# A second load of x under the gathered codes: the sum is made by the gathering DMA and copied by ScalarE instead of added by VectorE, and the orders of all engines are laid out anew

## The reference, cut to what matters

```
x = x + code(gn(x))          # layer 0: nearest of 1024 codes: argmin of the distance, then take(emb.T, index)
x = x + rows(gn(x))          # layer 1: sigmoid attention inside each row of 64 tokens
x = x + gate(gn(x)) * gn(x)  # layer 2: softmax over all 4096 tokens of an outer product, then a sigmoid gate
x = x + lin(gn(x))           # layer 3: linear attention with 4 heads, projection, layer norm
```

## Time and profile before

| | |
|---|---|
| median of three runs | 5602.64 us |
| profiled execution | span 5601.4 us from the first to the last instruction; the page gives no other time of it |
| TensorE matmul | 5252.2 us busy, 94% |
| VectorE | 4106.3 us, 73% |
| ScalarE | 3978.2 us, 71% |
| GpSimd | 1936.0 us, 35% |
| mean granted TensorE clock | 0.966 of full speed |
| mean DMA rate | 38 GB/s |

### The profile page before, as it was taken

The page is one execution under the profiler, slowest core; times in us unless marked ns, Lnnn a source line. Parts: engine busy times, 40 slices in busy tenths (PEclk is TensorE's granted clock), DMA queues, the critical chain, the costliest instruction groups (busy, mean ns, idle before and its releaser), DMA issues.

```text
span 5601.4 us, 113931 instructions
## 1 busy us (share of the span) xinstructions
PE 5252.2 (94%) x44520; PEld 2737.7 (49%) x44520; DVE 4106.3 (73%) x8674; ACT 3978.2 (71%) x6023; POOL 1936.0 (35%) x1594
## 2 busy tenths in 40 slices
PE   7799999999999999999999999999999999999996
PEld 3436445363553645446364453645436454463624
DVE  8467777776777777677777777777677777777726
ACT  1467867677785877868677675877858678686795
POOL 3225243342423424233352423424234242433403
PEclk9799999999999999999999999999999999999997
DMA  2010201102011020201102011020110102011000
GB/s 86 9 37 11 68 25 52 37 6 72 20 61 31 13 67 15 64 28 35 48 11 70 23 57 33 15 64 17 61 31 20 61 13 67 26 47 40 7 31 31
DMA packets 163253, 211.22 MB, mean 38 GB/s; under 512 B 13217, under 2 KB 146081, under 8 KB 162721
## 3 DMA queue, kind: packets, MB, share of 16 engines
q1 hardware_dynamic: 138144, 136.79, 7.6%
q0 software_dynamic: 24576, 67.14, 4.1%
HBM read 136.78 MB, written 67.11 MB: 36 GB/s over the span
## 4 chain that ended last, share of the span: by engine, by line
PE 66%; ACT 13%; DVE 11%; issue 6%; POOL 2%; DMA 1%; ACTq 0%; DVEq 0%; SPq 0%; POOLq 0%
PE PS L1195 33%; PE PS L1372 15%; PE PS L1363 6%; ACT n_x L529 3%; DVE stats L849 2%; PE PS L1471 2%; PE PS L1229 2%; PE PS L1253 2%; PE PS L1306 2%; ACT big L601 2%; ACT xin L529 2%; DMA quant_H<-emb_t,idx 1%; ACT work L568 1%; ACT attn L578 1%; ACT soft L601 1%
## 5 line engine op out<-in xcount | busy, mean ns | idle before, releaser
L601 ACT ACTIVATE big<-PS 128x1024 f32<-128x1024 f32 x1376 | 1365.8, 1024 | 460.3 <-PE PS L1363 398.9
L601 ACT ACTIVATE soft<-PS 128x1024 f32<-128x1024 f32 x672 | 676.2, 1024 | 353.9 <-PE PS L1363 346.3
L416 POOL DMA_INDIRECT quant_H<-emb_t,idx x512 | 487.4, 952 | 976.2 <-DVE idx L873 781.2
L1195 PE MATMUL PS<-e_hi,n_hi 128*128 128x512 f16 x2048 | 780.2, 381 | 17.3 <-DVE m L867 9.5
L1195 PE MATMUL PS<-e_hi,n_lo 128*128 128x512 f16 x2048 | 776.7, 379 | 0.0
L1195 PE MATMUL PS<-e_lo,n_hi 128*128 128x512 f16 x2048 | 776.7, 379 | 0.0
L1372 PE MATMUL PS<-big,w 128*4 128x512 f32 x5504 | 756.5, 638 | 0.0
L849 DVE BATCH_NORM_STATS2 stats<-XT 128x6 f32<-128x512 f32 x1024 | 651.7, 683 | 14.5 <-POOL XT L432 4.6
L873 DVE FIND_INDEX8 idx<-m,work 128x8 uint32<-128x1024 f32 x512 | 622.1, 1219 | 0.0
L1363 PE MATMUL PS<-rhs,lhs 12*128 12x512 bf16 x4096 | 557.6, 395 | 61.7 <-ACT big L601 38.8
L867 DVE CUSTOM_DVE_ANT_0 work<-PS,e_bias,m 128x512 f32<-128x512 f32 x512 | 384.0, 750 | 213.2 <-PE PS L1195 189.5
(11 more groups left out here) (208 smaller groups left out, 10799.7 us busy)
## 6 DMA issues: line engine op xcount, KB each, us to landing
xin<-x SPq DMA_DIRECT2D x128, 512.0 KB, 3.9
out<-yout SPq DMA_DIRECT2D x128, 512.0 KB, 2.9
quant_H<-emb_t,idx POOLq DMA_INDIRECT x512
XT<-emb SPq DMA_DIRECT2D x1, 1024.0 KB, 6.2
XT<-wh SPq DMA_DIRECT2D x1, 256.0 KB, 5.8
XT<-wqv SPq DMA_DIRECT2D x1, 256.0 KB, 5.8
XT<-wk SPq DMA_DIRECT2D x1, 128.0 KB, 5.8
w_sb<-w SPq DMA_DIRECT2D x1, 128.0 KB, 5.3
```

The source lines that it names most:

```text
L416: nc.gpsimd.indirect_dma_start(quant[:, g % 2, u, :], None, emb_t, bass.IndirectOffsetOnAxis(ap=idx[:, t % (2 * GT), 0:1], axis=0),).then_ ...
L601: nc.scalar.activation(E[h % 3][:, z * 1024:(z + 1) * 1024], bank(2 * z, 2), ACT.Exp).then_inc(exped.sem, 1)
L1195: ins = mm(dst, a, b, start=first and j == 0, stop=last and j == 2)
```

## The change

SyncE loads each group of x a second time, straight into `quant` (`x_again`). The gathering DMA adds the code rows to what lies there instead of writing over it. TensorE turns the sum as it turned the codes, and ScalarE copies the bank over `XT`; VectorE's `add0` is gone. GpSimd's gather now waits, at the first tile of a group, for the second load (`again`), and no longer for `l0_turned`; that wait is SyncE's. All lists are laid out anew, but TensorE's and GpSimd's for image 0 keep their order, and VectorE's for image 0 only loses `add0`.

```
+        again = [sem(f"again{s}") for s in range(2)]
 @block.sync
+            def x_again(im, g):
+                if g >= 2:
+                    sp.wait_ge(*l0_turned.after(im, 2 * g - 3))
+                elif im == 1:
+                    sp.wait_ge(*l1_outed.after(0, 2 * NG - 1))
+                elif im > 1:
+                    sp.wait_ge(*f_zed.after(im - 2, 2 * NG - 1))
+                sp.dma_start(quant[:, g % 2, :, :], xv[im, g]).then_inc(again[g % 2], 16)
             for new, old, last in images(B):
-                exp(old, 0, 0); final_out(last, 1); turn_in(new, 1); final_out(last, 3); turn_in(new, 3)
-                final_out(last, 5); turn_in(new, 5); final_out(last, 7); turn_in(new, 7); final_out(last, 9)
-                turn_in(new, 9); final_out(last, 11); final_out(last, 13); final_out(last, 15)
+                exp(old, 0, 0); final_out(last, 1); final_out(last, 3); turn_in(new, 1); final_out(last, 5)
+                turn_in(new, 3); final_out(last, 7); turn_in(new, 5); turn_in(new, 7); final_out(last, 9)
+                final_out(last, 11); final_out(last, 13); x_again(new, 0); turn_in(new, 9); x_again(new, 1)
+                x_again(new, 2); x_again(new, 3); final_out(last, 15); x_again(new, 4); x_again(new, 5)
+                x_again(new, 6); x_again(new, 7)
 @block.gpsimd
             def index(im, t):
                 g, u = t // GT, t % GT
-                pool.wait_ge(*l0_turned.room(im, t // 2, 4))
+                if u == 0:
+                    pool.wait_ge(again[g % 2], 16 * (im * NG // 2 + g // 2 + 1))
                 pool.wait_ge(*l0_indexed.after(im, t))
                 nc.gpsimd.indirect_dma_start(
                     quant[:, g % 2, u, :], None, emb_t,
-                    bass.IndirectOffsetOnAxis(ap=idx[:, t % (2 * GT), 0:1], axis=0),
+                    bass.IndirectOffsetOnAxis(ap=idx[:, t % (2 * GT), 0:1], axis=0), compute_op=ALU.add,
                 ).then_inc(gathered[g % 2][u], 16)
 @block.scalar
+            def add0(im, p):
+                g, c = p // 2, p % 2
+                here = XT[:, im % 2, :, g, c * 2 * P:(c + 1) * 2 * P]
+                act.wait_ge(*l0_turned.after(im, p))
+                nc.scalar.activation(here, bank(7).rearrange("p (k n) -> p k n", k=KC), copy).then_inc(l0_added.sem, 1)
 @block.vector
-            def add0(im, p):
-                g, c = p // 2, p % 2
-                here = XT[:, im % 2, :, g, c * 2 * P:(c + 1) * 2 * P]
-                dve.wait_ge(*l0_turned.after(im, p))
-                v.tensor_tensor(here, here, bank(7).rearrange("p (k n) -> p k n", k=KC), ALU.add).then_inc(l0_added.sem, 1)
```

More of the change, by code:

```diff
@@ L1108, in _ @@
[L1108 to L1114 removed]
+            turn_in(new, 5); turn_in(new, 6); turn_in(new, 7); turn_in(new, 8); turn_in(new, 9)
@@ new lines, in _ @@
+                fill(old, 7, 0); fill(old, 7, 1); sums(old, 5); final_z(last, 2); l3_qturn(last, 7)
+                fill(old, 8, 0); fill(old, 8, 1); final_out(last, 0); sums(old, 6); sums(old, 7)
+                fill(old, 9, 0); final_z(last, 3); turn_in(new, 0); fill(old, 9, 1); fill(old, 10, 0)
+                final_out(last, 1); sums(old, 8); final_z(last, 4); fill(old, 10, 1); fill(old, 11, 0)
+                turn_in(new, 1); final_out(last, 2); sums(old, 9); fill(old, 11, 1); fill(old, 12, 0)
@@ new lines, in _ @@
+                final_out(last, 3); final_z(last, 5); turn_in(new, 2); fill(old, 12, 1); sums(old, 10)
+                fill(old, 13, 0); turn_in(new, 3); final_z(last, 6); fill(old, 13, 1); final_out(last, 4)
+                sums(old, 11); fill(old, 14, 0); fill(old, 14, 1); final_out(last, 5); sums(old, 12)
+                fill(old, 15, 0); final_out(last, 6); final_z(last, 7); turn_in(new, 4); sums(old, 13)
+                fill(old, 15, 1); fill(old, 16, 0); sums(old, 14); turn_in(new, 5); final_z(last, 8)
@@ new lines, in _ @@
+                fill(old, 16, 1); fill(old, 17, 0); sums(old, 15); fill(old, 17, 1); final_out(last, 7)
+                final_z(last, 9); sums(old, 16); fill(old, 18, 0); fill(old, 18, 1); turn_in(new, 6)
+                final_z(last, 10); sums(old, 17); fill(old, 19, 0); fill(old, 19, 1); sums(old, 18)
+                final_out(last, 8); fill(old, 20, 0); turn_in(new, 7); final_z(last, 11); final_out(last, 9)
+                fill(old, 20, 1); fill(old, 21, 0); sums(old, 19); turn_in(new, 8); final_z(last, 12)
@@ new lines, in _ @@
+                final_out(last, 10); fill(old, 21, 1); fill(old, 22, 0); sums(old, 20); turn_in(new, 9)
+                final_z(last, 13); fill(old, 22, 1); fill(old, 23, 0); sums(old, 21); final_out(last, 11)
+                turn_in(new, 10); fill(old, 23, 1); sums(old, 22); final_out(last, 12); final_z(last, 14)
+                turn_in(new, 11); fill(old, 24, 0); fill(old, 24, 1); sums(old, 23); turn_in(new, 12)
+                final_out(last, 13); fill(old, 25, 0); final_z(last, 15); fill(old, 25, 1); sums(old, 24)
@@ new lines, in _ @@
+                fill(old, 26, 0); final_out(last, 14); fill(old, 26, 1); sums(old, 25); fill(old, 27, 0)
+                turn_in(new, 13); fill(old, 27, 1); final_out(last, 15); fill(old, 28, 0); turn_in(new, 14)
+                fill(old, 28, 1); sums(old, 26); fill(old, 29, 0); fill(old, 29, 1); turn_in(new, 15)
+                sums(old, 27); fill(old, 30, 0); fill(old, 30, 1); sums(old, 28); fill(old, 31, 0)
+                fill(old, 31, 1); gn(new, 0, 1); sums(old, 29); gn(new, 0, 2); fill(old, 32, 0)
@@ new lines, in _ @@
+            final_out(last, 9); fill(old, 14, 1); fill(old, 15, 0); sums(old, 12); sums(old, 13)
+            fill(old, 15, 1); final_z(last, 13); final_out(last, 10); fill(old, 16, 0); fill(old, 16, 1)
+            sums(old, 14); final_z(last, 14); fill(old, 17, 0); fill(old, 17, 1); sums(old, 15)
+            final_out(last, 11); fill(old, 18, 0); sums(old, 16); fill(old, 18, 1); fill(old, 19, 0)
+            fill(old, 19, 1); final_out(last, 12); sums(old, 17); fill(old, 20, 0); fill(old, 20, 1)
```

806 lines of the change are left out of this document (360 added, 446 removed).

## The result

The changed kernel takes 5730.94 us, the median of four runs (5725.98 to 5732.52), beside 5603.25 us for the kernel before on the same chip (four runs, 5601.81 to 5604.72). The ratio is 1.0231, with a 95% interval of 1.0216 to 1.0245: 2.3% slower, 128 us. I had said 5590, between 5556 and 5630.

What follows compares the result with a forecast made beforehand. TensorE was taken to bound the loop and VectorE image 0; -0.25 us a pass times 15 (-3.8) and -8.2 in image 0 gave -12.0, so 5590 us, with 5556 to 5630 to hold 8 times in 10.

Steps and rivals of the forecast that it cites:

- x: Extra time of an adding gather over a plain one: 0.5 us forecast, bounds 0 and 3.5.
- -10.7 in image 0: Image 0, where VectorE was taken as the bound: removing 16 add0 steps of 0.67 us saves 10.7 us.
- all other reorderings: Start of the fills, layers 1 and 3, image 15: same instructions, put at 0, 1 us a pass either way.
- Two are close: In the loop only turn0(0) and turn0(15) stand close enough behind their index for a slower gather to cost.
- VectorE's relief, -0.7 us a pass: Loop, score stretch: add0 leaving VectorE gains 0.7 us a pass through small holes, ends 0 and 3.
- Image 0, -8.2 in all: Image 0: 10.7 us gained from VectorE's removed add0, less 2.5 us for slower gathers.
- 5x = 2.5: Image 0: the slower gather costs at four turns and at the end, five times 0.5 us.
- my formula: Slower gathers cost x at two turns a pass and five times in image 0, 35 times in all.
- Rival 1: The adding gather is slow, TensorE stands at turn0(0) and turn0(15): 5626 us with x = 1.5; chance 0.28.
- turn0(0) and turn0(15), 1.4 and 0.65: Loop, first and last gather-dependent turns: costs of 0.9 + x = 1.4 and 0.15 + x = 0.65 us a pass.
- The norm of layer 0, -2.0: Loop, between the last turn of x and the first score: 2.0 us a pass gained, bounds 1.0 and 2.7.
- SyncE's list, 0.4: Loop: load of group 7, behind a second load and a store, comes late for turn_in(14): 0.4 us a pass lost.

Runs made afterwards that it cites:

- e1: Changed kernel's lists and copy on ScalarE, but plain overwriting gather and no second load of x, result lacks x in layer 0: 5650.14 us, 1.0074.
- e7: Kernel before with only the changed TensorE and ScalarE lists around the norm of layer 0: 5606.96 us, 1.0010.
- e4: Kernel before, own lists, with one change: the gather adds to quant, which is loaded once at the start: 5681.21 us, 1.0141.
- e9: Kernel before with 16 fills a pass moved by half a score in the score stretch, same instructions: 5702.70 us, 1.0180.
- e3: Changed kernel with the adding gather, but quant loaded only once at the start and the gather waiting for l0_turned again: 5725.36 us, 1.0217.
- e6: Changed kernel with the load of group 7 moved ahead of two stores and x_again(new, 0) in SyncE's list: 5696.47 us, 1.0171.
- e10: Kernel before, own mechanism, with the changed lists from the beginning of a loop pass to the first score: 5625.74 us, 1.0040.
- e11: Kernel before, own mechanism, with the changed lists from the norm of layer 1 to the end of the pass: 5624.04 us, 1.0040.

## Why the prediction was wrong, point by point

*The two steps that failed.* With x at 0 and no second load, my own terms put the new lists alone at some 35 us less than before (-1.65 a pass and -10.7 in image 0). Measured (e1) they are 44 us more: the largest error, 79 us. It is made of a relief of which no pass shows anything, of a norm stage whose gain e7 finds worth nothing, and of "all other reorderings", which I had put at 0. The second is the price of the adding gather: 35 x 0.5 = 17.5 us forecast, 69 to 80 measured. There it was the count of turns that wait, "Two are close", that failed first, and x only after it: in e4 five turns of a pass wait, and in image 0 of the changed kernel seven ahead of the last.

*What bounds the kernel.* Right: TensorE in the loop (a pass takes 339.0 us in the mean, where the one that I had read took 338). But I read its lists as a sum of durations that doesn't depend on order, and e9 shows that it does.

*VectorE's relief, -0.7 us a pass.* Nothing came. From the first turn0 to the last score TensorE is idle for 0.25 us a pass before; there was no hole to give back. The relief shows as idle time of VectorE, whose waits for scores grew from 429 to 624 us. Image 0, -8.2 in all: the first layer 1 starts 2.0 us later instead. Two rows of VectorE, changed kernel, four tiles apart:

```profile
74.02 1.22 DVE L902 FIND_INDEX8 idx<-m,work 128x8 uint32<-128x1024 f32 x1
...
85.88 0.75 DVE L896 CUSTOM_DVE_ANT_0 work<-PS,e_bias,m 128x512 f32<-128x512 f32 x1 [0.30 <-PE PS L1215]
...
86.75 1.22 DVE L902 FIND_INDEX8 idx<-m,work 128x8 uint32<-128x1024 f32 x1
```

They are 12.73 us apart, where I had 11.8. With VectorE at 9.3 and TensorE at 9.0 of 10 us neither is full: VectorE waits 0.3 at a time for scores, and TensorE 0.76 for a gather (84.00, below). Further on the gathers stand one behind the other on GpSimd, 1.55 us each, and TensorE stands longer:

```profile
84.00 0.44 PE L1273 MATMUL PS<-ident,quant_H 128*128 128x128 f32 x2 [0.76 <-DMA quant_H<-emb_t,idx]
...
126.27 1.55 POOL L431 DMA_INDIRECT quant_H<-emb_t,idx  x1 [0.30 <-issue]
128.13 1.55 POOL L431 DMA_INDIRECT quant_H<-emb_t,idx  x1 [0.31 <-issue]
130.21 0.44 PE L1273 MATMUL PS<-ident,quant_H 128*128 128x128 f32 x2 [1.45 <-DMA quant_H<-emb_t,idx]
```

Ahead of the last turn, image 0's waits for gathers are 6.7 us at seven turns (4, 7, 8, 9, 11, 12, 14), where the kernel before has 0.25 at one. By my own sign, that image 0 gains nothing, the prediction is wrong in its reasons too. Without the mechanism image 0 gains 4.7 us (e1: layer 1 at 161.9), not 10.7, and adding takes 9.4 in the changed lists (e3 at 171.3), where I had 5x = 2.5.

*The gather, x = 0.5.* It was 1.05 from the gather's start, inside its bounds and past the 0.84 from which I had the kernel slower. My value took the DMA engines' time (0.45 became 0.94: that half was right) and left out that GpSimd issues it 0.6 us longer. From the end of the index, from where my formula counts, only 0.55 are left, since the gather without the wait for `l0_turned` starts sooner; that I had not foreseen, and that 0.5 comes near to it is luck. Even 1.05 would by my formula have given only 35 x 0.55 = 19 us more, 5610. The formula failed in its other half, "Two are close": in e4 five turns of a pass wait, since I had counted the distance from the end of the index and not from where GpSimd gets to the gather, behind the norm and other gathers. In the changed lists the waits are 0.9 at turn0(0), 0.8 at turn0(8) and 1.2 at turn0(15), 2.9 a pass in all, and 0.5 for GpSimd's norm, which stands behind longer gathers. Rival 1, with 0.28, named the mechanism, and the sign I had given for it (a pass above 339 us with waits for the gather) is what the profile shows; its price was less than half of the measured one.

*turn0(0) and turn0(15), 1.4 and 0.65.* Their waits came out near: 0.9, and 1.2 against 0.5 before. One slip: I counted two fills as 0.66 us where the earlier trace rows has 0.33 for both. At turn0(0) it stands on both sides and cancels; it made turn0(15) 0.33 us too dear and the gain at the norm 0.33 too small.

*The norm of layer 0, -2.0.* The stage shrank by 1.8 to 2.3 as worked out, and e7 shows that this is worth nothing: a stage between two cuts isn't a path. I had counted moved work as gained, and not asked what the earlier exp(32,0) and the moved fills do to the stage ahead.

*SyncE's list, 0.4 (ends 0 and 1.6; 5.9 against 5.4 would have been 0.5).* The wait was 1.3, and in e6 a pass without it is 2.3 shorter. The load landed 5.7 us after its issue, not the 4.9 that I had; so the Trainium skill's rule that queues interleave on the same engines ("DMA: Bandwidth & Descriptors", Issuing engines are not separate DMA queues), which I had put beside the sum at 0.8, was the nearer guess.

*All other reorderings, 0 with 1 us either way.* 44 us more with the mechanism off, 4.2 a pass in the profile, though image 0 gains 5 in it. I had checked that the instructions are the same and that TensorE is full before and after. Both are true, and both are true of e9 too, which is 100 us slower. Of the 4.2 us a pass in e1, 1.3 are more idle time, spread over the pass, and none is the clock. The changes of weight shape would be 1.6 by their count, but where they lie doesn't fit where the loss is (e10, e11), so the cause of this loss is not settled. The largest growth, 2.6 us a pass from start to start, part of it idle time, is behind the last products of qv and k in layer 3, and e11, which has those lists alone, shows the same 2.6.

The Trainium skill's adder in line with the stream ("DMA: Bandwidth & Descriptors", SDMA does more than copy) left only the second read as a cost. The engines' 0.49 us more a gather don't contradict it; the longer hold of the issuing engine, 0.62 us beside a lateness of 1.05, stands outside that rule.

## What to carry to other kernels

Price a longer DMA by every consumer whose slack is smaller than the added latency, counted from the engine that issues it and its queue, not from the producer; here 1 us on every gather was 4 to 5 us a pass in either set of lists. Ask also which waits the issuing step loses or gains: one wait less gave back half of that microsecond. When TensorE is full, "the same instructions in another order" is not zero: count the small matmuls that are split from their neighbours and the changes of weight shape, and expect a tuned order to lose by a move more often than to gain. Look at the granted clock of every run beside its waits: here the time at 1.2 GHz was an estimated 1.2 of 9.1 us a pass in the changed kernel, and 1.9 of 5.1 in e4. A relief of an engine pays only where the bound engine has a hole, and a stage that gets shorter has gained only what the whole pass gains.

## What the runs showed of the hardware

- Small matmuls at different row offsets overlap: four of 12 rows and 512 columns at four offsets take 0.33 us, two alone 0.32.
- A score matmul is followed by another after 0.215 us, by one with weights of 12x128 or 128x4 after 0.31, but by a float32 turn with 128x128 weights after 0.215.
- An indirect gather of 128 rows of 1 KB that adds holds GpSimd 1.56 us instead of 0.94, has 144 packets instead of 48, takes the DMA engines 0.94 us instead of 0.45, and lands 3.9 us after issue (changed kernel) instead of 2.7 (e1_neither).
- With GpSimd idle, a gather starts 0.27 us after the index it waits for where its step has that wait alone, and 0.76 to 0.77 us after it where a second wait stands ahead of it (medians of 95 to 178 gathers a run).
- TensorE's busy time rose by 93 us over fourteen passes in e9 with no more work in it: a full engine in the profile is not a useful one.
